# Opening of a convolution-attention hybrid: where its 0/1 blocks, first constants, weight products and shift rows are handled

## The chip, the cores and the metric

One core of a Trainium2 chip. The metric is the device time of one execution in microseconds. TensorE does matrix products into PSUM, ScalarE activations and copies, VectorE elementwise work and reductions, GpSimd (POOL) fills and casts, SyncE (SP) issues DMAs; ScalarE can issue DMAs too. Each engine runs its own instructions in order and waits for others at semaphores.

## The reference

The input is `x`, 4 images of 64 channels by 1,024 positions. Layer 0 is per image, over the 1,024 positions as tokens:

```
x_ln = layernorm(x over channels) * ln1_w + ln1_b
q, k, v = x_ln @ qkv_w            # 4 heads of 16
x = x + proj(softmax(q k^T / 4) v) + proj_b
x = x + fc2(gelu(fc1(layernorm(x) * ln2_w + ln2_b)))
```

Layer 1 takes the result `t` as tokens: a second attention of 8 heads of 64 over a sliding window of 32 tokens, `t + (attention @ Wu^T + bu)`, then a batch-normed linear layer with a recurrence over the images' tokens, `y = sigmoid(wx + y V^T)`, added to `t`. In layer 1 the products of weights `Wq^T Wk` and `Wv^T Wu^T` are formed once for each head and used in place of the four matrices.

## The kernel before

**Tiling.** Channels lie on partitions, and an image's 1,024 positions are two halves of 512 columns, one on partitions 0 to 63 and one on 64 to 127. Matmuls have 512 columns. PSUM has eight banks: `T` (three), `O`, `R` (four).

**The attention of layer 0.** Keys and queries are split in three bf16 parts (`qk_part`), and rows of these parts are stacked to 96 rows (`KX`, `QX`), so that one bf16 matmul gives scores near fp32. For each image and half a first pass computes all scores only for their row maxima (`max_piece`: a matmul at L795 into a bank of a ring, a VectorE reduction at L1308), 32 pieces with 8 for each head. `max_end` then negates (`max_neg`), transposes (`max_rows`, L804) and splits the maxima in three parts (`max_parts`); SyncE copies those to three more rows of `QX` (`shift_rows`, L607 to L612, three transfers), where rows of ones in `KX` add them to the scores. Then `scores` (L815), the exponential on ScalarE (L1146) and `values` (L830) run over 16 key blocks (`u`) and 4 heads.

**The opening.** Image 0 has no time for a trip through DRAM, so `relay` (L774) stacks its rows with matmuls against 0/1 blocks `sel`, which ScalarE makes in twelve copies of `eye` (L1216 to L1219). SyncE issues image 0, `first` (all constants that layer 0 opens with, 714 columns), `early`, `rest`, and the other images (L577 to L581). POOL fills `eps`, `sel` with zeros, the value tiles `VT` with zeros and then ones, others, and the rows of ones in `KX` (L646 to L659); ScalarE waits for the fifth of these that is counted before its table load (L1212). The norm is `ln_mean` (L721), `ln_square` (L1104), `ln_var` (L727, L1109, L1111), `ln_scale` (L1270). Filler matmuls (`keep_clock`, L696) stand before waits of TensorE: seven at the very start, five before the first `ln_var`, eight before the first projection. The projection (L741) is evicted by ScalarE at L1122. Images 1 to 3 have their rows split by POOL and stacked through DRAM (`relayout`, L583).

**Products.** `products` forms two folded bias columns, the products of `Wq`, `Wk` into `R` (`abd`), those of `Wv`, `Wu` into `O` (`gbd`), and a third folded column; ScalarE copies them out.

**The order.** One list, `timeline`, names all steps, and each engine runs those that it has. `order_of_stages` writes it: the opening by hand (L219 to L223), with the relay of the next head after piece 3 of each head and `products` at that place of the last; then the 284 steps of `attend_stages` of four images, among which tables of places put the maxima of the next half (`MAX_AT`), all steps of layer 0's rest and layer 1 (`LAYER_AT`, in quarters of a step), and the end (`END_AT`, `UNIFY_AT`). A plan of the PSUM ring (`plan_ring`) follows from the list.

## Time and profile before

| | us |
|---|---|
| median of 3 runs | 460.96 |
| lowest, highest | 454.33, 461.22 |
| the profiled execution | 458.44 |
| its span | 456.5 |
| TensorE busy | 413.2 |
| VectorE busy | 296.7 |
| ScalarE busy | 296.3 |
| POOL busy | 42.3 |

The span runs from the first to the last instruction of one profiled execution; 1.9 us of its time lie around it. Timelines and windows count from the span's start. A row of a timeline merges equal neighbours (`x7`), and the bracket at its end is the idle time of that engine before it and what ended it. An fp32 matmul is recorded as two instructions.

### The profile page before, as it was taken

The numbers are of one execution on the slowest core, as the hardware profiler recorded it, in microseconds if no ns is written. First come the engines' busy times: TensorE is split into PE (matmuls) and PEld (weight loads), VectorE is DVE, ScalarE is ACT, GpSimd is POOL, SyncE is SP. The second block draws the span as 40 slices with busy tenths as digits, with TensorE's granted clock in tenths as the row PEclk, the third lists the DMA queues.
The fourth block names the chain that finished last, engine by engine and source line by source line (L and its number), as shares of the span: only waits on it lengthen the run. The fifth ranks groups of instructions, "written<-read, shape, count | busy, mean of one in ns | idle before, by whom it ended". The sixth has DMA issues, their size and how long they took to land.

```text
span 456.5 us, 7908 instructions
## 1 busy us (share of the span) xinstructions
PE 413.2 (91%) x3210; PEld 156.6 (34%) x3210; DVE 296.7 (65%) x541; ACT 296.3 (65%) x512; POOL 42.3 (9%) x57
## 2 busy tenths in 40 slices
PE   6787999999999999999999999899999988897893
PEld 2335232322322433232224433232134322453492
DVE  1696795989998746579885556997042644625424
ACT  3442577758788477587876675779977756264551
POOL 9300110003003000012031000000300000100000
PEclk9997699999999999999999999999999999799997
DMA  7300065001810000005500000000000000000003
GB/s 294 99 1 1 3 130 79 12 2 23 183 16 1 14 1 1 1 13 128 81 3 13 1 1 3 12 2 1 1 3 1 0 1 0 3 1 2 1 1 93
DMA packets 7158, 14.02 MB, mean 31 GB/s; under 512 B 1872, under 2 KB 4176, under 8 KB 6992
## 3 DMA queue, kind: packets, MB, share of 16 engines
q1 hardware_dynamic: 7120, 13.50, 12.7%
q8 instruction: 26, 0.43, 0.4%
q14 instruction: 12, 0.10, 0.1%
HBM read 9.20 MB, written 3.41 MB: 28 GB/s over the span
## 4 chain that ended last, share of the span: by engine, by line
PE 63%; ACT 15%; DVE 13%; issue 3%; DMA 3%; POOL 2%; SPq 1%; DVEq 0%; ACTq 0%; POOLq 0%
PE O L830 10%; PE T L815 5%; DVE part_max L1308 5%; PE T L795 5%; ACT z L1169 4%; PE R L815 3%; PE R L727 3%; PE R L999 3%; PE R L886 3%; PE R L795 3%; PE R L960 3%; PE R L721 2%; PE R L987 2%; DMA KX<-qk_scratch 2%; PE R L974 2%
## 5 line engine op out<-in xcount | busy, mean ns | idle before, releaser
L1308 DVE TENSOR_REDUCE part_max<-T 128x1 f32<-128x512 f32 x164 | 105.7, 683 | 23.4 <-PE T L795 23.1
L1146 ACT ACTIVATE probs<-T 128x512 f32<-128x512 f32 x146 | 81.3, 601 | 23.4 <-PE T L815 23.1
L1146 ACT ACTIVATE probs<-R 128x512 f32<-128x512 f32 x110 | 62.2, 599 | 19.2 <-PE R L815 18.9
L830 PE MATMUL O<-probs,VT 128*32 128x512 f32 x512 | 67.6, 603 | 0.3 <-ACT probs L1146 0.2
L1308 DVE TENSOR_REDUCE part_max<-R 128x1 f32<-128x512 f32 x92 | 60.7, 683 | 10.0 <-PE R L795 9.5
L795 PE MATMUL T<-KX,QX 96*128 96x512 bf16 x164 | 57.0, 393 | 4.6 <-DVE part_max L1308 3.0
L815 PE MATMUL T<-QX,KX 99*128 99x512 bf16 x146 | 49.6, 384 | 1.8 <-DVE part_max L1308 1.3
L815 PE MATMUL R<-QX,KX 99*128 99x512 bf16 x110 | 38.1, 382 | 0.6 <-DVE qk_rest L1285 0.4
L672 POOL CAST zs<-z 128x512 bf16<-128x512 f32 x28 | 17.2, 614 | 200.6 <-ACT z L1169 200.6
L795 PE MATMUL R<-KX,QX 96*128 96x512 bf16 x92 | 32.7, 387 | 1.8 <-DMA KX<-qk_scratch 0.9
L1177 ACT ACTIVATE p<-R 128x1024 f32<-128x1024 f32 x14 | 14.3, 1024 | 26.7 <-PE R L960 26.7
L795 PEld LDWEIGHTS T<-KX,QX 96*128 96x128 bf16 x164 | 15.0, 99 | 47.8 <-DVE part_max L1308 18.6
L1169 ACT ACTIVATE z<-R 64x512 f32<-64x512 f32 (+1 forms) x44 | 26.2, 596 | 5.6 <-PE R L886 4.6
L815 PEld LDWEIGHTS T<-QX,KX 99*128 99x128 bf16 x146 | 12.6, 97 | 38.1 <-ACT probs L1146 12.5
L1430 DVE TENSOR_TENSOR zs<-R,rden 128x512 f32<-128x512 f32 x24 | 15.4, 685 | 13.4 <-PE R L987 13.4
L1104 ACT ACTIVATE ln_q<-R 128x512 f32<-128x512 f32 (+1 forms) x14 | 8.2, 589 | 20.6 <-PE R L721 20.6
L886 PE MATMUL R<-xp,abd 64*64 64x512 f32 x128 | 17.2, 613 | 2.4 <-ACT z L1169 2.1
L1184 ACT ACTIVATE rlog<-R 128x1024 f32<-128x1024 f32 x16 | 16.3, 1020 | 4.7 <-PE R L974 4.6
L830 PEld LDWEIGHTS O<-probs,VT 128*32 128x32 f32 x512 | 10.3, 108 | 26.4 <-issue 15.8
L1400 DVE TENSOR_REDUCE neg_m<-R 128x16 f32<-128x576 f32 x16 | 12.1, 758 | 10.5 <-PE R L921 10.5
L815 PEld LDWEIGHTS R<-QX,KX 99*128 99x128 bf16 x110 | 9.7, 97 | 24.5 <-issue 6.4
L727 PE MATMUL R<-ln_q,s_first 128*128 128x512 f32 (+1 forms) x28 | 16.1, 660 | 2.1 <-ACT ln_q L1104 2.1
(241 smaller groups left out, 592.8 us busy)
## 6 DMA issues: line engine op xcount, KB each, us to landing
qk_scratch<-qk_part SPq DMA_DIRECT2D x12, 192.0 KB, 3.0
zs<-early SPq DMA_DIRECT2D x1, 2048.0 KB, 8.4
QX<-qk_scratch SPq DMA_DIRECT2D x6, 256.0 KB, 5.4
KX<-qk_scratch SPq DMA_DIRECT2D x6, 256.0 KB, 5.7
result<-probs SPq DMA_DIRECT2D x2, 512.0 KB, 5.1
s_rest<-rest SPq DMA_DIRECT2D x1, 946.0 KB, 11.1
X<-x SPq DMA_DIRECT2D x2, 384.0 KB, 12.6
QX<-qk_scratch SPq DMA_DIRECT2D x6, 128.0 KB, 5.5
```

The lines of the kernel that those rows point to most:

```text
L672: nc.gpsimd.tensor_copy(*z_cast_of(h)).then_inc(g["z_cast"], 1)
L727: mm(ln_bank(b, which, i, 1), t["mean_c"], ln_bufs(b, which, i)["ln_q"], start=True, stop=True).then_inc(g["ln_var"], 1)
L795: mm(ring["max_piece", b, half, i], QX[b % 2][0:KQ, half, h, nt * P:(nt + 1) * P], KX[b % 2][0:KQ, kh, h, :], start=True, stop=True).then_ ...
L815: mm(ring["scores", b, u, h], KX[b % 2][:, j // QT, h, j % QT * P:(j % QT + 1) * P], QX[b % 2][:, half, h, :], start=True, stop=True).then ...
L830: last = mm(O[h * HP:(h + 1) * HP, :], VT[b % 2][:, j, h, :], probs[:, u % 2, h, :], start=(j == 0), stop=(j == KT - 1))
L886: last = mm(R[half_rows(half ^ odd), (h + odd) % z_banks(b), :], abd[half_rows(half), h + odd, half_rows(half)], xn[half_rows(half), :], s ...
L1146: A(probs[:, u % 2, h, :], ring["scores", b, u, h], ACT.Exp, scale=HD ** -0.5).then_inc(g["exp_done"], 1)
L1169: last = A(dst, ps, ACT.Copy)
L1177: A(p1[:, r % 2, :, :], s1_bank(b, r), ACT.Exp).then_inc(g["p1_exp"], 1)
L1184: A(rlog[:, :, :], den1_bank(b, r), ACT.Ln).then_inc(g["den1_log"], 1)
L1308: nc.vector.tensor_reduce(part_max[:, row, kh:kh + 1], ring["max_piece", b, half, i], AX_X, ALU.max).then_inc(g["max_red"], 1)
L1430: last = TT(cols, pv1_bank(b, r)[odd].rearrange("p (k h q) -> p k h q", k=PPS, h=H1), rden1(b, r)[:, odd, :].rearrange("p (k h q) -> p k h ...
```

## The change

- The twelve copies that make the 0/1 blocks go from ScalarE's start to behind its last activation of the first norm (`rows_of_parts`).
- `first` is cut in two: `first` (`mean_c`, `center`, vectors; 266 columns), issued by ScalarE, and `second` (`eye`, `wq`, `wk`, `wv`; 448 columns), issued by SyncE at the old place. TensorE waits for `second` before the bias matmuls.
- ScalarE's table load waits for one POOL fill instead of five. The two zero fills of `VT` go; POOL's counts fall by two.
- Two filler matmuls instead of five stand before the first `ln_var`.
- `products` is two steps. The first (two folds, `abd`) stands after the fourth piece of the last head instead of the third, the second (`gbd`, last fold) after the eighth.
- The shift rows of a half go in one transfer instead of three.
- The four tables of places have new values (the first of each is shown).

```diff
-FIRST = {"mean_c": P, "center": P, "vectors": len(VECTORS), "eye": C, "wq": P, "wk": P, "wv": P}
+FIRST = {"mean_c": P, "center": P, "vectors": len(VECTORS)}
+SECOND = {"eye": C, "wq": P, "wk": P, "wv": P}
...
 MAX_AT = (
     (
-        0, 0, 0, 0, 1, 1, 1, 6, 6, 7, 8, 8, 10, 10, 11, 12, 13, 15, 15, 15, 15, 16, 21, 21, 21, 21, 21, 22, 24, 29, 34),
+        0, 0, 1, 1, 2, 3, 4, 4, 6, 7, 7, 7, 7, 10, 10, 13, 13, 15, 16, 18, 18, 18, 18, 18, 18, 18, 18, 25, 29, 29, 33),
...
 LAYER_AT = (
-    0, 0, 0, 2, 5, 5, 15, 320, 320, 320, 322, 332, 335, 339, 344, 344, 346, 359, 383, 396, 405, 406, 411, 413,
+    0, 0, 0, 3, 9, 9, 17, 320, 320, 320, 323, 324, 333, 341, 344, 344, 346, 357, 373, 397, 408, 408, 413, 415,
...
-        out += [*pieces[:RELAY_AT], ("relay", 0, h + 1) if h + 1 < H0 else ("products",), *pieces[RELAY_AT:]]
+        out += [*pieces[:RELAY_AT], *([("relay", 0, h + 1), *pieces[RELAY_AT:]] if h + 1 < H0 else [pieces[RELAY_AT], ("products", 0), *pieces[RELAY_AT + 1:], ("products", 1)])]
...
             load_x(0, 1, "x0_in")
-            sp.dma_start(pack["first"][:], a["first"]).then_inc(g["first_in"], 16)
+            sp.dma_start(pack["second"][:], a["second"]).then_inc(g["second_in"], 16)
             sp.dma_start(pack["early"], a["early"]).then_inc(g["early_in"], 16)
...
-                for p in range(PARTS):
-                    sp.dma_start(QX[b % 2][KQ + p:KQ + p + 1, half, :, :].rearrange("o h (t n) -> o (h t) n", n=P),
-                                 mx_part[p * ROWS:(p + 1) * ROWS, :]).then_inc(g["shift_in"], 16)
+                sp.dma_start(QX[b % 2][KQ:KQ + PARTS, half, :, :].rearrange("p h (t n) -> p (h t) n", n=P),
+                             mx_part[:, :]).then_inc(g["shift_in"], 16)
...
             for i in range(2):
-                nc.gpsimd.memset(VT[i][:], 0.0).then_inc(g["pool_fills"], 1)
-            pool.wait_ge(g["pool_fills"], 3)
-            for i in range(2):
                 nc.gpsimd.memset(VT[i][:, :, :, HD:HP], 1.0).then_inc(g["pool_fills"], 1)
...
                 if which == 1 and b < 1:
-                    keep_clock(5)
+                    keep_clock(2)
...
                 if b < 1:
                     keep_clock(8)
+                    pe.wait_ge(g["second_in"], 16)
...
+            def rows_of_parts():
+                act.wait_ge(g["sel_zero"], 1)
+                act.wait_ge(g["second_in"], 16)
+                for q in range(2):
+                    for i, r in enumerate(PART_OF_ROW[q]):
+                        last = A(sel[:, q, r, i, :], t["eye"], ACT.Copy)
+                last.then_inc(g["sel_done"], 1)
...
                 A(buf["ln_r"], buf["ln_l"], ACT.Exp, scale=-0.5).then_inc(g["ln_rstd"], 1)
+                if (b, which) == (0, 1):
+                    rows_of_parts()
...
-            act.wait_ge(g["pool_fills"], 5)
+
+            act.dma_start(pack["first"][:], a["first"]).then_inc(g["first_in"], 16)
+            act.wait_ge(g["pool_fills"], 1)
             nc.scalar.preload_act_table_set("natural_log_exp_and_others")
-            act.wait_ge(g["sel_zero"], 1)
-            act.wait_ge(g["first_in"], 16)
-            for q in range(2):
-                for i, r in enumerate(PART_OF_ROW[q]):
-                    last = A(sel[:, q, r, i, :], t["eye"], ACT.Copy)
-            last.then_inc(g["sel_done"], 1)
```

## Rows read from the trace of the kernel before

**Rows 1.** The page: TensorE's busy tenths in 40 slices, then its granted clock.

```profile
PE   6787999999999999999999999899999988897893
...
PEclk9997699999999999999999999999999999799997
```

**Rows 2.** Window 80 to 380 us: busy (instructions) of PE, PEld, DVE, ACT, POOL; clock.

```profile
80.00:380.00 300.00, 286.58 (x2216) 93.97 (x2213) 208.85 (x369) 221.28 (x357) 21.66 (x32) 1.00 0.10 20
```

**Rows 3.** Chain of waits, opening: start, length, what.

```profile
6.93 1.86 ACT z L1218 x12
...
22.37 12.06 DVE part_max L1308 x20
```

**Rows 4.** Timeline of TensorE, 0 to 11 us: start, length, instruction, idle before.

```profile
1.99 3.01 PE L700 MATMUL T<-abd 128*128 128x512 bf16 x7 [1.99 <-DVE abd L1452]
5.95 1.10 PE L721 MATMUL R<-X,s_first 128*128 128x512 f32 x2 [0.95 <-DMA s_first<-first]
6.89 1.24 PE L700 MATMUL T<-abd 128*128 128x512 bf16 x5
9.33 1.13 PE L727 MATMUL R<-ln_q,s_first 128*128 128x512 f32 x2 [1.20 <-ACT ln_q L1104]
```

**Rows 5.** Timeline of ScalarE, 0 to 16 us.

```profile
5.64 1.28 ACT L1213 ACT_TABLE_LOAD   x1 [5.64 <-POOL VT L652]
...
8.70 0.57 ACT L1104 ACTIVATE ln_q<-R 128x512 f32<-128x512 f32 x1
...
13.97 1.27 ACT L1122 ACTIVATE qk_part<-R,qk_bias 128x512 bf16<-128x512 f32 x2 [2.13 <-PE R L741]
```

**Rows 6.** Timeline of POOL: the first fill that is counted.

```profile
0.74 0.10 POOL L646 MEMSET eps<- 128x1 f32 x1 [0.29 <-POOLq L1605]
```

**Rows 7.** DMA issues: KB each, median us from issue to landing.

```profile
s_first<-first SPq DMA_DIRECT2D x1, 357.0 KB, 3.8
X<-x SPq DMA_DIRECT2D x2, 128.0 KB, 2.7
```

**Rows 8.** Timeline of TensorE, 34 to 50 us.

```profile
34.71 0.34 PE L1017 MATMUL R<-s_first 128*128 128x1 f32 x2
...
36.94 1.93 PE L1027 MATMUL O<-zs 128*64 128x64 f32 x32
...
43.01 0.66 PE L804 MATMUL T<-s_rest,neg_max 128*48 128x128 f32 x2 [2.40 <-DVE neg_max L1313]
...
45.28 1.92 PE L721 MATMUL R<-X,s_first 128*128 128x512 f32 x2
47.88 2.07 PE L727 MATMUL R<-ln_q,s_first 128*128 128x512 f32 x2 [0.69 <-ACT ln_q L1104]
```

**Rows 9.** Timeline of VectorE, 34 to 41 us.

```profile
34.94 1.88 DVE L1308 TENSOR_REDUCE part_max<-T 128x1 f32<-128x512 f32 x3
39.47 0.69 DVE L1308 TENSOR_REDUCE part_max<-R 128x1 f32<-128x512 f32 x1 [2.65 <-PE R L795]
```

**Rows 10.** Windows of 2 us, columns as in rows 2.

```profile
34.00:36.00 2.00, 1.79 (x22) 1.41 (x23) 2.00 (x4) 0.32 (x2) 0.00 (x0) 0.86 0.00 0
...
38.00:40.00 2.00, 2.00 (x23) 1.22 (x20) 0.53 (x1) 1.48 (x3) 0.00 (x0) 0.79 0.00 0
...
42.00:44.00 2.00, 0.99 (x3) 0.37 (x4) 1.20 (x5) 0.00 (x0) 0.00 (x0) 0.57 0.00 0
```

**Rows 11.** Shift: issue, waiting matmul, queue from 44 to 50 us, landing; TensorE's waits.

```profile
100.85 1.79 SPq L611 DMA_DIRECT2D QX<-mx_part  x3
...
103.84 0.61 PE L815 MATMUL R<-QX,KX 99*128 99x512 bf16 x2 [0.20 <-DMA QX<-mx_part]
...
q1 hardware_dynamic: 96, 0.01, 1.2%
...
QX<-mx_part SPq DMA_DIRECT2D x3, 4.0 KB, 1.8
...
PE R L795 <- DMA KX<-qk_scratch: 0.9, 1, 0.9
```

## The prediction and its working

> **What bounds the kernel.** I read the page's slices first. From the fifth to the thirty-sixth TensorE is busy 8 or 9 tenths of each; the first four and the last four are looser, and the granted clock is down in slices four and five (34 to 57 us) and near the end [rows 1]. A window puts a number on the middle: between 80 and 380 us TensorE stands idle 300 - 286.6 = 13.4 us, with VectorE busy 209 of 300 [rows 2]. So the middle is a full TensorE queue, which passes on whatever happens ahead of it: what the opening gains, the end gains. The change works on the opening (0 to 53 us), and there the chain of waits says what sets the time: ScalarE's twelve copies are on it, then the first norm, and from 22.4 to 34.4 us VectorE's row maxima, back to back [rows 3]. The timelines fill in the rest, with what each engine waited for.
>
> **Start of the first norm.** TensorE's seven filler matmuls end at 5.00 us; it then waits 0.95 us for the first constants, and centres the image at 5.95 us [rows 4]. ScalarE can't use that at once: it waits for POOL's fifth counted fill until 5.64, loads its table for 1.28, makes the twelve 0/1 blocks (1.86 us) and squares at 8.70 us [rows 3, 5]. TensorE stands 1.20 us before the variance matmul at 9.33 [rows 4]. The change does three things here.
> First, the copies go behind the norm's second activation. Second, the table load waits for one POOL fill, done at 0.84 us, not for five [rows 6]. Third, `mean_c`, `center` and the vectors (266 of 714 columns, 136 KB of 357 KB) leave on ScalarE's own queue while SyncE issues the image. Today they are issued third, at 5.84 - 3.8 = 2.04 us; the two 128 KB image halves, of the same size and issued before that, land 2.7 us after issue, so by 4.7 us [rows 4, 7]. ScalarE has nothing else to do, so it issues near 0.8 us, as POOL's first fill starts; I expect the 136 KB near 0.8 + 2.7 = 3.5 us and bound it by 0.8 + 3.8 = 4.6. All are inside the fillers, so the centring starts at 5.00. It takes 1.10 us; the square takes 0.57 and TensorE starts 0.06 us behind it (9.33 - 9.27), with as much ahead of it. The variance matmul starts at 5.00 + 1.10 + 0.04 + 0.57 + 0.05 = 6.76 against 9.33: **2.57 us**. Five fillers take 1.24 us [rows 4], so two take 0.5 and end inside the 0.66 us in between: the smaller number costs nothing.
> The copies now lie between the norm's last activation and the first projection eviction at 13.97, an idle of 2.13 us in which VectorE scales and TensorE projects [rows 5]. They take 1.86: 0.27 us of slack, and beyond it only the excess would cost. Their reader, the relay, stands behind that eviction and two VectorE steps. `wq`, `wk`, `wv`, `eye` (229 KB) hold SyncE's old third place and land by 5.8 us as the bigger transfer does now; their first reader, the bias matmuls, stands behind eight fillers after 6.76 + 1.1 us. SyncE issues as many as before. The two full fills of `VT` go; POOL sets nothing in the opening but the table load. Bounds of this part: 0.95 us less if the constants are as late as now; 0.8 us less if TensorE's matmuls are still slow at 5.0 us (the seven fillers take 0.43 us each, the next five 0.25 [rows 4]).
>
> **Products of weights.** They now stand after three pieces of the last head's maxima. From 34.71 us on folds and `abd` take 2.23 us, then `gbd` 1.93, then the last fold about 0.3 [rows 8]. VectorE, back to back so far, runs out at 36.82 and waits 2.65 us [rows 9]. After the change a fourth piece goes ahead, into the bank that VectorE leaves at about 35.0, then folds and `abd` until 37.5, and the next piece is there at 37.9. VectorE has four pieces, until 36.82 + 0.6 = 37.4: it waits 0.5 us, not 2.65. That is **2.1 us** (2.65 if `abd` runs at full clock). The `gbd` part follows the eighth piece. TensorE now stands 2.40 us behind that piece, for VectorE's maxima and `neg_max` [rows 8]; after the change VectorE has four pieces until 37.9 + 2.4 = 40.3 and the negation until 40.7, and TensorE works until 40.3 to 40.5, so nothing is added. At half clock pieces and `gbd` end near 41.5, 0.8 us too late: then the term is 1.3. ScalarE's copies of `gbd`, which the second norm waits for through the last fold, end about 1.5 us after TensorE's part, at 41.9, and that norm would start near 42.2; behind them ScalarE has only that norm.
>
> **The clock.** Behind the 2.40 us of idle the granted clock falls: 0.57 in the window from 42 to 44 us [rows 10], and slice five (to 57 us) shows 6 tenths [rows 1]. Transposing and four pieces take 45.28 - 43.01 = 2.27 us here, the centring 1.92 and the variance 2.07 [rows 8], where the first norm has 1.10 and 1.13 at full clock [rows 4]. At twice the clock the first would be up to 1.1 shorter; I take 0.8, since the ring's fourth bank is held by the transposed maxima until VectorE has read it. Sum: 0.8 + 0.82 + 0.94 = **2.6 us**. With the gap filled by `gbd`, I take the clock to stay up: it rose within 38 to 40 us, right after products and folds alone [rows 10], and was at full from slice one to three with pieces and relay. Against it: it fell within 34 to 36 us, where TensorE was busy 1.79 of 2 us [rows 10].
>
> **Shift transfer.** SyncE issues three today, over 1.79 us, and the last lands 103.84 - 100.85 = 2.99 us after the first issue. TensorE is idle for it there for 0.20 us [rows 11]; I saw no other place in the waits. One transfer has the same 48 pieces of 256 bytes; it lands 1.8 us after issue plus what its spread costs. The four denominator transfers queued behind it on SyncE go 1.2 us sooner. At most **0.2 us**, and not below -1.
> The spread: three issues moved 96 packets in 1.2% of 16 engines' 6.0 us [rows 11], or 1.15 us, 24 ns for each that carries data. If one transfer ran on three engines, 16 would stand in a row: 0.4 us, landing at 2.2 us, still 0.8 sooner. The Trainium skill, DMA: Bandwidth & Descriptors, section "Why a DMA increments its semaphore by 16 and not by 1", speaks against the edit: the engines used are the largest number that divides the slowest dimension of both sides, by which this one has 3 of 16 (3 and 48), and each of today's three has 16. With the row's price the sum by that rule keeps its 0.2; no run here shows it yet.
>
> **Orders.** The tables of places move most maxima and layer steps of the middle by a few places. Counts are the same. There are 13.4 us of idle to win from or add to; I take 0 and bounds of 3 either way. The wait of 0.9 us for the keys of image 1 [rows 11] stays, since both its sides move together; the projection is placed one score later, 0.2 to 0.4 us.
>
> **Sum.** The profiled execution took 458.44 us, 456.5 of it span, 0.5% under the median of 460.96; one of three runs was at 454.33. 458.44 - 2.57 - 2.1 - 0.2 - 2.6 = 451.0 us.
>
> **Rivals.**
> - The clock falls all the same. For it: it fell once in a busy stretch. Then 458.44 - 2.57 - 1.3 - 0.2 = 454.4 us.
> - The gain is taken back in the middle: TensorE is early at some transfer or VectorE (209 of 300 us busy, but near its limit wherever maxima stand close) has no room. The wait for the keys of image 1 would grow, or the orders lose 3 us: 455 to 460, say 457.
> - Orders that also win: 3 us more, 448. For it, the 13.4 us; against it, that is 4% of 300 and split over many waits.
> - The other side, slower than before: the new order misplaces maxima so that TensorE stands before VectorE's banks between 80 and 380 us. Idle there would have to go from 13.4 to above 21 us to use up the 7.5 gained, and to 33 us for 2% slower. A wait there is a VectorE reduction's length, 0.6 us (12.06 for 20 [rows 3]), so it takes 13 of them to lose the gain; at 18 the time is 462 us.
> - The one transfer is served by three engines, and a packet in a row costs far more than 24 ns: at 0.13 us each (an assumed price) it lands at 1.8 + 16 x 0.13 = 3.9 us, 0.9 later than today, and TensorE waits that at the one place: 451.0 + 0.2 + 0.9 = 452.1 us. The page of the Trainium skill just named would bring it about.
>
> **Chances.** My sum 0.48; clock falls 0.22; taken back 0.12; orders win 0.10; slower 0.05; three engines dear 0.03. The likeliest one's own range is 448.5 to 453.5. For 8 in 10, I go from 447.5 (the winning orders, nearly whole) to 457.5 (half of what is taken back). A change of 2%, about what a measurement of this kernel can tell from none, is 9.2 us: below 451.7. A bit over half of the sum's case (0.28), the winning orders (0.10) and a little of the three-engine one (0.01) lie there: 0.39. Slower by over 2% (470.2) keeps 0.03, the rest 0.58.
>
> **What would show it.** Centring at 5.0 and variance matmul at 6.8 us; ScalarE's twelve copies before an eviction at 11.4; VectorE's gap in the last head at most 0.6 us; `neg_max` near 38.1; no granted clock of 0.50 from 40 to 50 us, and a second norm whose matmuls take 1.1 each; the variance matmul of the second norm near 41.6, not 47.9. Wrong would be: constants landing after 5.0, idle in 80 to 380 us far from 13.4, or the shift waited for by more than 1 us.

## The result, and the profile after

The changed kernel takes 451.25 us (median of 4 runs, 450.95 to 452.19). The kernel before, run beside it on the same chip, took 461.09 us (four runs, 454.33 to 462.95). The ratio is 0.9894 with an interval of [0.9848, 0.994]: 1.1% faster, and the same within 2%. A ratio leaves out executions more than 1.5% above a kernel's fastest, here two of before's four (461.22 and 462.95), so that one of the two left is its shortest, 454.33; the medians of all four differ by 9.84 us, 2.1%.

The time itself came out as predicted (451.0), the change of it did not: -2.2% was forecast against the median of three, -1.1% measured. A second comparison, below (six runs beside eleven of before), gave 0.9847 [0.9801, 0.9894]. Beside the experiments before ran 83 times (453.05 to 462.84, median 458.3), and the changed kernel ran 10 times in all (448.99 to 453.89, median 451.3): 7.0 us, or 1.5%, less. Whether one reads 1.1, 1.5 or 2.1% depends on which runs of before one meets, and that is the subject of what follows.

The page of the changed kernel, TensorE's busy tenths and granted clock in 40 slices. Slices four and five are up against [rows 1]; the fall near the end is still there.

```profile
PE   7789999999999999999999999899999888897893
...
PEclk9998999999999999999999999999999999699997
```

TensorE of the changed kernel in the opening, answering to [rows 4]: start, length, instruction, idle before. Then ScalarE, answering to [rows 5].

```profile
1.99 3.17 PE L697 MATMUL T<-abd 128*128 128x512 bf16 x7 [1.99 <-DVE abd L1462]
4.95 1.91 PE L718 MATMUL R<-X,s_first 128*128 128x512 f32 x2
...
7.55 1.13 PE L724 MATMUL R<-ln_q,s_first 128*128 128x512 f32 x2
```

```profile
0.74 0.38 ACTq L1227 DMA_DIRECT2D s_first<-first  x1
1.15 1.28 ACT L1229 ACT_TABLE_LOAD   x1 [1.15 <-POOL eps L646]
...
9.97 1.85 ACT L1108 ACTIVATE z<-s_second 128x64 bf16<-128x64 f32 x12
12.19 1.27 ACT L1133 ACTIVATE qk_part<-R,qk_bias 128x512 bf16<-128x512 f32 x2 [0.37 <-PE R L739]
```

The centring starts behind the fillers without a wait, at 4.95, and the variance matmul at 7.55, where it was at 9.33. The centring took 1.91 us, not 1.10, as a matmul of its size does at half clock. (The granted clock of the windows says 1.00 in these first microseconds all the same, in every profile here, so the mean granted clock used below doesn't count a slow start.) The twelve copies run at 9.97, and the eviction behind them still waits 0.37 us for TensorE, so they cost nothing.

TensorE and VectorE of the changed kernel at the last head and the second norm, answering to [rows 8] and [rows 9].

```profile
34.10 1.73 PE L1022 MATMUL R<-zs 128*64 128x64 f32 x32
...
37.58 1.26 PE L1028 MATMUL O<-zs 128*64 128x64 f32 x32
...
39.35 0.42 PE L802 MATMUL T<-s_rest,neg_max 128*48 128x128 f32 x2 [0.20 <-DVE neg_max L1323]
...
40.75 1.08 PE L718 MATMUL R<-X,s_first 128*128 128x512 f32 x2
42.51 1.13 PE L724 MATMUL R<-ln_q,s_first 128*128 128x512 f32 x2 [0.69 <-ACT ln_q L1113]
```

```profile
34.95 0.68 DVE L1318 TENSOR_REDUCE part_max<-R 128x1 f32<-128x512 f32 x1
36.41 1.89 DVE L1318 TENSOR_REDUCE part_max<-T 128x1 f32<-128x512 f32 x3 [0.77 <-PE T L793]
...
38.92 0.37 DVE L1323 TENSOR_REDUCE neg_max<-part_max 128x16 f32<-128x32 f32 x3
```

VectorE waits 0.77 us where it waited 2.65, TensorE 0.20 where it waited 2.40, and the second norm's matmuls take 1.1 us each where they took 1.92 and 2.07. Its variance matmul stands at 42.51, before at 47.88.

Windows of the changed kernel, columns as in [rows 2]. The clock still falls at `abd`, as it did before (0.61 from 34 to 36 us; 0.86 and then 0.50 in before); from 42 to 44 us it is full, where before had 0.57. The middle has 15.8 us of idle against 13.4.

```profile
34.00:36.00 2.00, 2.00 (x35) 1.75 (x35) 1.63 (x3) 0.46 (x3) 0.00 (x0) 0.61 0.00 0
...
42.00:44.00 2.00, 1.49 (x5) 0.68 (x6) 1.60 (x4) 0.78 (x2) 0.00 (x0) 1.00 0.03 6
...
80.00:380.00 300.00, 284.20 (x2200) 93.86 (x2200) 204.81 (x364) 220.60 (x354) 22.45 (x33) 1.00 0.09 19
```

The shift transfer, answering to [rows 11]: its issue on SyncE, the weight load that waits for it, and the hardware queue from 40 to 46 us, in which one shift is sent.

```profile
93.12 0.78 SPq L611 DMA_DIRECT2D QX<-mx_part  x1
```

```profile
95.41 0.23 PEld L813 LDWEIGHTS R<-QX,KX 99*128 99x128 bf16 x2 [0.54 <-DMA QX<-mx_part]
```

```profile
q1 hardware_dynamic: 51, 0.01, 0.9%
```

It lands by 95.41, 2.29 us after its issue (before 2.99); the forecast for three engines was 2.2.

### The profile page after: what moved, and what is told of

The parts are those of the page before. It is cut to its first block, busy times and chain, and to the rows that moved or that the text cites. A ratio compares the mean times of both kernels' runs of the same rounds, so it can differ in the third digit from the quotient of the medians.

```text
span 449.2 us, 7886 instructions
## 1 busy us (share of the span) xinstructions
PE 410.0 (91%) x3207; PEld 155.4 (35%) x3207; DVE 296.0 (66%) x541; ACT 296.4 (66%) x512; POOL 40.7 (9%) x55
## 4 chain that ended last, share of the span: by engine, by line
PE 66%; ACT 18%; DVE 12%; issue 3%; DVEq 0%; ACTq 0%
PE O L828 11%; PE T L813 6%; DVE part_max L1318 5%; ACT z L1182 5%; PE T L793 5%; PE R L813 4%; ACT probs L1159 4%; PE R L793 4%; PE R L997 3%; PE R L958 3%; PE R L718 3%; PE R L724 3%; PE R L884 2%; PE R L985 2%; PE R L972 2%
## 5 line engine op out<-in xcount | busy, mean ns | idle before, releaser
L1318 DVE TENSOR_REDUCE part_max<-T 128x1 f32<-128x512 f32 x160 | 103.1, 681 | 16.7 <-PE T L793 16.3
L1159 ACT ACTIVATE probs<-T 128x512 f32<-128x512 f32 x151 | 84.4, 599 | 20.7 <-PE T L813 20.2
L1159 ACT ACTIVATE probs<-R 128x512 f32<-128x512 f32 x105 | 59.5, 601 | 20.1 <-PE R L813 19.5
L1318 DVE TENSOR_REDUCE part_max<-R 128x1 f32<-128x512 f32 x96 | 62.8, 681 | 4.6 <-PE R L793 4.4
L793 PE MATMUL T<-KX,QX 96*128 96x512 bf16 x160 | 55.0, 387 | 4.4 <-DVE part_max L1318 2.1
L813 PE MATMUL T<-QX,KX 99*128 99x512 bf16 x151 | 51.8, 383 | 2.3 <-DVE part_max L1318 2.3
L813 PE MATMUL R<-QX,KX 99*128 99x512 bf16 x105 | 36.2, 382 | 0.0
L813 PEld LDWEIGHTS T<-QX,KX 99*128 99x128 bf16 x151 | 13.4, 97 | 41.3 <-DVE part_max L1318 16.5
L972 PE MATMUL R<-p,s_rest 64*64 64x512 f32 x128 | 17.0, 599 | 0.8 <-ACT rlog L1197 0.4
```

Of the source, the lines that this page charges most:

```text
L793: mm(ring["max_piece", b, half, i], QX[b % 2][0:KQ, half, h, nt * P:(nt + 1) * P], KX[b % 2][0:KQ, kh, h, :], start=True, stop=True).then_ ...
L813: mm(ring["scores", b, u, h], KX[b % 2][:, j // QT, h, j % QT * P:(j % QT + 1) * P], QX[b % 2][:, half, h, :], start=True, stop=True).then ...
L972: last = mm(den1_bank(b, r)[half_rows(half), odd, :], t["block_ones"][half_rows(odd), :], p1[half_rows(odd), r % 2, half, :], start=True, ...
L1159: A(probs[:, u % 2, h, :], ring["scores", b, u, h], ACT.Exp, scale=HD ** -0.5).then_inc(g["exp_done"], 1)
L1318: nc.vector.tensor_reduce(part_max[:, row, kh:kh + 1], ring["max_piece", b, half, i], AX_X, ALU.max).then_inc(g["max_red"], 1)
```

## The experiments

All times are in us. "At equal clock" is explained under the second group. The short names in bold are used afterwards.

### Each part alone

**Start alone**: before, with the two transfers, the copies behind the norm, one fill awaited, POOL's two zero fills gone, and two fillers.

```diff
-FIRST = {"mean_c": P, "center": P, "vectors": len(VECTORS), "eye": C, "wq": P, "wk": P, "wv": P}
+FIRST = {"mean_c": P, "center": P, "vectors": len(VECTORS)}
+SECOND = {"eye": C, "wq": P, "wk": P, "wv": P}
...
-                    keep_clock(5)
+                    keep_clock(2)
...
+                if (b, which) == (0, 1):
+                    rows_of_parts()
...
+            act.dma_start(pack["first"][:], a["first"]).then_inc(g["first_in"], 16)
+            act.wait_ge(g["pool_fills"], 1)
```

> The kernel before with the first part alone: constants in two transfers, copies behind the norm's second activation, table load after one fill, two fillers; products, shift and places as before. By my sum the variance matmul of the first norm starts 1.8 to 2.6 us sooner and the whole kernel ends that much sooner: 456 us against a profiled 458.4. The clock's fall behind the idle stretch at 40 us stays. The rival (the part is given back in the middle) says no change.

454.85 (452.29 to 459.82, 10 runs), ratio 0.9946 [0.9898, 0.9994]. In its profile the centring takes 1.30, the variance matmul starts at 6.94 (2.39 earlier), and nothing else changes: the gaps of 2.65 and 2.40 us are there, and the clock falls behind them as before. TensorE, and the window from 42 to 44 us:

```profile
40.61 0.66 PE L803 MATMUL T<-s_rest,neg_max 128*48 128x128 f32 x2 [2.40 <-DVE neg_max L1324]
...
42.89 1.91 PE L719 MATMUL R<-X,s_first 128*128 128x512 f32 x2
```

```profile
42.00:44.00 2.00, 2.00 (x5) 0.82 (x3) 1.96 (x5) 0.00 (x0) 0.00 (x0) 0.50 0.01 2
```

**Products alone**: before, with the products in two parts.

```diff
-        out += [*pieces[:RELAY_AT], ... else ("products",), *pieces[RELAY_AT:]]
+        out += [*pieces[:RELAY_AT], ... else [pieces[RELAY_AT], ("products", 0), *pieces[RELAY_AT + 1:], ("products", 1)]]
```

> The kernel before with the products in two parts and nothing else. By my sum VectorE's gap in the last head falls from 2.65 to at most 0.8 us and TensorE's idle before the transposed maxima from 2.40 to under 0.5 us; the clock then stays up in the second norm, whose centring takes 1.1 instead of 1.9 us: 2.1 + 2.6 = 4.7 us less than the profiled before, near 453.7. The rival (the clock falls all the same) says 2.1 or less, 456 to 457, with 0.50 in the windows of 42 to 50 us.

452.82 (451.25 to 454.73, 4 runs), ratio 0.9891 [0.9783, 0.9998]. Run again:

> The kernel before with the products in two parts, once more. By the traces of the run with the gap filled, VectorE's gap at full clock is 1.14 us, not 2.65; so the split is worth 0.5 to 0.9 us against runs of before at the same clock, and the rest of its gain is that its clock stays up more often: mean clock above 0.98 in most runs, median 453 to 454.5. My recorded terms (2.1 at equal clock) say 2 us under before's runs of the same clock.

454.01 (451.09 to 457.58, 12 runs), ratio 0.9914 [0.9879, 0.9949]. VectorE, then TensorE, of the first of the two:

```profile
40.87 1.29 DVE L1313 TENSOR_REDUCE part_max<-T 128x1 f32<-128x512 f32 x2 [1.15 <-PE T L795]
```

```profile
38.32 1.98 PE L1024 MATMUL R<-zs 128*64 128x64 f32 x32
...
43.82 0.42 PE L804 MATMUL T<-s_rest,neg_max 128*48 128x128 f32 x2 [0.59 <-DVE neg_max L1318]
...
45.22 1.07 PE L721 MATMUL R<-X,s_first 128*128 128x512 f32 x2
```

TensorE waits 0.59 us, not 2.40, and the second norm runs at full clock. VectorE's gap was to be at most 0.8 us and is 1.15, with the first part of the products at half clock (1.98); in the second of the two profiles, at full clock, it has none. TensorE and the second norm do what was expected, start or no start.

**New opening, old places** (the changed kernel with the four tables of before), and **old opening, new places** (the reverse):

```diff
-MAX_AT, LAYER_AT, END_AT, UNIFY_AT as in the changed kernel
+MAX_AT, LAYER_AT, END_AT, UNIFY_AT as in the kernel before
```

> The changed kernel with the four tables of places of the kernel before. My sum puts nothing on the tables: 451 to 452 us, as the changed kernel. If the tables carry part of the gain, it is slower than the changed kernel by that part; the wait for the keys of image 1 near 70 us, gone in the changed kernel, would be back with 0.9 us.

453.14 (450.24 to 455.58, 4 runs), ratio 0.9885 [0.9779, 0.9992]. Its profiled execution is its longest, 455.58, with a mean clock of 0.973. TensorE never waits ahead of the transposing there, and yet it is at half clock from the products to the second norm's centring:

```profile
40.15 0.66 PE L802 MATMUL T<-s_rest,neg_max 128*48 128x128 f32 x2
...
42.42 1.59 PE L718 MATMUL R<-X,s_first 128*128 128x512 f32 x2
```

```profile
38.00:40.00 2.00, 2.00 (x34) 1.88 (x32) 1.41 (x5) 0.25 (x1) 0.00 (x0) 0.50 0.01 4
```

> The kernel before with the new tables of places alone. My sum: no change (within 1 us of before). If the tables alone gain, up to 1 to 2 us less than before.

457.57 (455.94 to 461.26, 10 runs), ratio 1.0011 [0.9967, 1.0056]. The profiled execution of this one matters later: its opening is before's, instruction for instruction up to the last head, with a mean clock of 0.979. TensorE, VectorE, and a window:

```profile
35.29 1.15 PE L1022 MATMUL R<-zs 128*64 128x64 f32 x32
36.27 1.10 PE L1027 MATMUL O<-zs 128*64 128x64 f32 x32
...
41.51 0.42 PE L804 MATMUL T<-s_rest,neg_max 128*48 128x128 f32 x2 [2.40 <-DVE neg_max L1313]
```

```profile
37.96 0.69 DVE L1308 TENSOR_REDUCE part_max<-R 128x1 f32<-128x512 f32 x1 [1.14 <-PE R L795]
```

```profile
42.00:44.00 2.00, 2.00 (x6) 0.67 (x4) 1.90 (x6) 0.00 (x0) 0.00 (x0) 0.73 0.00 0
```

TensorE was at full clock at the products here, undivided as they are. They take 1.15 and 1.10 us, not the 1.88 and 1.93 of before's profile [rows 8], and VectorE waits 1.14 us for them, not the 2.65 of [rows 9]. The clock falls only later, behind the 2.40 us of idle.

Then the first of the two again:

> The changed kernel with the tables of places of before, once more with more rounds (4 runs gave 450.2 to 455.6). My sum: within 0.5 us of the changed kernel in the median. The rival (the new places carry part of the gain) says 1 us or more slower, as the wait for the keys of image 1 comes back.

451.51 (448.73 to 455.79, 6 runs), ratio 0.9824 [0.9771, 0.9877]. So the new tables gain nothing: alone they change nothing in the ratio, and the new opening is at least as good without them, though TensorE then does stand for the keys of image 1 (TensorE of the first run with the old places; no matmul of the changed kernel has such a wait):

```profile
72.33 0.60 PE L793 MATMUL R<-KX,QX 96*128 96x512 bf16 x2 [1.43 <-DMA KX<-qk_scratch]
```

### Filling TensorE's gap without moving anything

The runs of each kernel of the first group spread by 3 to 8 us, and so the spread was larger than the effects. It isn't the chip: before ran beside the others on five of them, with medians from 457.9 to 458.5 and 5.8 us or more from lowest to highest on each. Sorted by the mean granted clock that each run shows, before's 83 runs fall almost on a line (some of the clocks):

| mean granted clock | runs of before | median us |
|---|---|---|
| 0.987 | 4 | 453.2 |
| 0.983 | 5 | 455.1 |
| 0.980 | 4 | 455.7 |
| 0.975 | 12 | 456.9 |
| 0.972 | 9 | 458.1 |
| 0.968 | 13 | 459.6 |
| 0.965 | 3 | 460.8 |
| 0.964 | 7 | 461.1 |
| 0.961 | 1 | 462.8 |

The line through all 83 has a slope of -0.34 us for each 0.001 of clock, with 0.47 us of scatter around it. A kernel's distance to this line, at its own clock, is what it gains "at equal clock"; the rest of its gain is a higher clock. The two add up to the whole by the way they are defined, and the line credits a higher clock wherever it is gained, also where it buys no time. Only 10 of the 83 runs have 0.983 or more; the profiled one has 0.972, the median. If the gap ahead of the second norm makes the difference, ten fillers in it should bring the long runs down and leave the shortest alone.

**Gap filled**: before, with ten dependency-free matmuls on data of the kernel ahead of the wait for `neg_max`.

```diff
             def max_rows(b, half):
 
+                if b == 0 and half == 0:
+                    pe.wait_ge(g["abd_done"], 4)
+                    keep_clock(10, pack["rest"][:, 0:256].bitcast(BF16), O[:, :])
                 pe.wait_ge(g["negmax"], 2 * b + half + 1)
```

> The kernel before with ten filler matmuls into bank O while TensorE waits for the negated maxima of the first half (2.40 us of idle at 40.6 us); nothing else changed. If the idle stretch is what lets the clock fall there, the clock stays at full from 40 to 53 us, the second norm's centring takes 1.1 instead of 1.9 us, and the kernel is 2 to 2.6 us shorter than before though no work moved. If the clock's fall has another cause, the windows still show 0.50 and the time is that of before or up to 0.5 us more.

454.86 (453.36 to 456.53, 8 runs), ratio 0.9938 [0.9899, 0.9977]; before had 458.21 beside it (25 runs, 453.19 to 461.61). The median is 3.3 lower, the fastest run is not; at equal clock it is 0.4 worse, though in the profile the fillers delay nothing (the transposing starts at 41.49, with the gap left idle at 41.51). The spread is down from 8.4 in 25 runs to 3.2 in 8. Its TensorE:

```profile
38.98 2.33 PE L700 MATMUL O<-s_rest 128*128 128x512 bf16 x10
...
42.89 1.08 PE L721 MATMUL R<-X,s_first 128*128 128x512 f32 x2
```

**Start filled** and **both filled**: 9 and 10 fillers around the first norm where before has 7 and 5; and both together.

```diff
-            keep_clock(7)
+            keep_clock(9)
...
-                    keep_clock(5)
+                    keep_clock(10)
```

> The kernel before with nine fillers instead of seven at the start and ten instead of five before the first variance matmul, so that TensorE never waits long in the first 9 us. The runs of before lie between 454 and 463 us, those of the changed kernel within 1.3 us. Theory: before's spread comes from where the clock rises in an opening with two idle stretches; then this kernel's highest run comes down by some us and its median is below that of before by 1 to 3 us. Rival: the spread comes from the later fall of the clock or from transfers; then the spread stays 5 us and more.

458.83 (453.24 to 461.44, 12 runs), ratio 0.9984 [0.9949, 1.002].

> Both sets of fillers. If the clock alone makes the spread, this one has runs within 1.5 us of one another and a median near the lowest run of before, 454 us. If not, the spread stays.

455.13 (453.52 to 459.34, 12 runs), ratio 0.9948 [0.9916, 0.9981]. Filling around the first norm brings nothing; filling the gap ahead of the second brings 3 us on the median. The runs with both filled were to lie within 1.5 us of one another and span 5.8, so that gap is a large source of the spread and not the only one. The profiles show two more. With the start filled, with both filled and in the first run of products alone the clock goes to half between 20 and 21 us, for 3 to 4 us, while TensorE relays the second head. In five profiles (start alone, gap filled, products alone again, three shifts, and one of the last group) it is at half for 3 to 4 us between 288 and 296. Neither is in the profiles of before or of the changed kernel. Both filled, then gap filled:

```profile
22.00:24.00 2.00, 2.00 (x9) 0.53 (x6) 0.43 (x2) 1.20 (x3) 0.00 (x0) 0.50 0.00 0
```

```profile
292.00:294.00 2.00, 2.00 (x12) 0.52 (x12) 1.93 (x4) 1.23 (x4) 0.00 (x0) 0.50 0.00 0
```

The profiles put the stretches side by side. The first goes from the first norm's variance matmul to the transposing of `neg_max`, the second from there to the second norm's variance matmul; the last column is from the same transposing to the projection of image 1.

| profile | products | clock at products | first stretch | second stretch | to projection |
|---|---|---|---|---|---|
| before | undivided | half (1.88, 1.93) | 33.68 | 4.87 | 9.44 |
| start alone | undivided | half (1.98, 1.80) | 33.67 | 4.88 | 9.42 |
| start filled (half clock at the relay) | undivided | half (1.78, 1.93) | 35.29 | 4.87 | 9.43 |
| old opening, new places | undivided | full (1.15, 1.10) | 32.18 | 4.08 | 8.69 |
| gap filled | undivided | full (1.15, 1.10) | 32.16 | 3.17 | 6.55 |
| both filled (half clock at the relay) | undivided | full (1.15, 1.10) | 33.29 | 3.17 | 6.55 |
| changed | divided | half, then nearly full (1.73, 1.26) | 31.80 | 3.16 | 6.55 |
| three shifts | divided | half (1.98, 1.97) | 32.94 | 3.23 | 6.62 |
| new opening, old places | divided | half (1.98, 1.98) | 32.96 | 4.54 | 7.93 |
| products alone (half clock at the relay) | divided | half, then full (1.98, 1.15) | 34.11 | 3.16 | 6.54 |
| products alone, again | divided | full (1.15, 1.15) | 31.01 | 3.16 | 6.55 |
| tail filled (below) | divided | full (1.15, 1.15) | 31.00 | 3.17 | 6.55 |

Dividing saves 33.68 - 32.94 = 0.7 us with both at half clock and 32.17 - 31.01 = 1.2 with both at full; the clock at the products saves 1.5 by itself undivided and 1.9 divided. Half clock at the relay costs 1.6 (start filled against before) or 1.1 (both filled against gap filled). In all four profiles that keep the gap the clock falls behind it; with the gap filled, by fillers or by `gbd`, the way to the projection is 2.1 to 2.9 us shorter in every profile but one. That one is the new opening with old places: its clock was down at the products and came up only at 43 us.

### The shift transfer

**Three shifts**: the changed kernel with before's three transfers.

```diff
-                sp.dma_start(QX[b % 2][KQ:KQ + PARTS, half, :, :].rearrange("p h (t n) -> p (h t) n", n=P),
-                             mx_part[:, :]).then_inc(g["shift_in"], 16)
+                for p in range(PARTS):
+                    sp.dma_start(QX[b % 2][KQ + p:KQ + p + 1, half, :, :]..., mx_part[p * ROWS:(p + 1) * ROWS, :])
```

> The changed kernel with three shift transfers a half, as before. My sum gives the single transfer 0.2 us: this one is 0 to 0.3 us slower than the changed kernel. The rule that a transfer of 3 rows is served by three engines says the single one lands with 16 packets in a row; the trace of the changed kernel against this one shows whose last packet comes sooner after the first issue (three: 2.99 us).

451.95 (450.94 to 454.58, 6 runs), ratio 0.9849 [0.9812, 0.9886]. The changed kernel again, later:

> The changed kernel itself, next to the kernels beside it. Theory (a run's time is set by where its clock is down): its runs lie 4 us under runs of before that have the same mean granted clock (0.983: 455 for before, 451 for this), and its fastest runs show a clock of 0.98 and more. The ratio to before lies between 0.984 and 0.990. If the clock did not matter, runs of equal clock would differ as widely as all do.

451.98 (448.99 to 453.89, 6 runs), ratio 0.9847 [0.9801, 0.9894]. The waits for this transfer differ as expected (the page's waits: total, times, longest; three transfers first, then one), and no difference in time is to be seen. (Before has such waits of its weight loads too, 1.4 and 0.9 us; the prediction counted the matmul's 0.20 alone.)

```profile
PEld R L814 <- DMA QX<-mx_part: 1.8, 2, 1.2
...
PEld T L814 <- DMA QX<-mx_part: 1.0, 2, 0.8
```

```profile
PEld T L813 <- DMA QX<-mx_part: 0.8, 1, 0.8
...
PEld R L813 <- DMA QX<-mx_part: 0.5, 1, 0.5
```

### Towards a better kernel

**Tail filled**: the changed kernel, with fillers ahead of and between the window products of the last image, where the clock falls in every kernel above. **Early and tail**: that, with TensorE starting 0.8 us sooner and a filler behind each of three pieces of the last head.

```diff
                 for k in range(2):
+                    if b == B - 1:
+                        keep_clock(1, ones16)
                     bank = win_bank(b, r)[:, k, :]
...
                 if r == 0:
+                    if b == B - 1:
+                        keep_clock(6, ones16)
                     pe.wait_ge(g["xbd_cast"], b + 1)
```

> The changed kernel with six filler matmuls before and one within each of the eight window groups of the last image, where every run so far shows 7 to 10 us of half clock. If the idle and the small matmuls there let the clock fall, it stays up longer and the kernel is 1 to 2.5 us shorter than the changed one; if not, the fillers cost up to 1 us.

452.17 (451.79 to 455.81, 6 runs), ratio 0.9875 [0.9831, 0.9919].

> The same with two more edits in the opening: the fill that the first fillers read is cut, so that TensorE starts at about 1.3 instead of 2.0 us and centres the first image near 4.5 instead of 5.0; and one filler behind each of three pieces of the last head. Theory: 0.5 to 1 us less than the kernel with the tail filled alone. Rival: the image lands too late for that, no difference.

452.11 (450.85 to 453.10, 6 runs), ratio 0.9844 [0.9806, 0.9882]. TensorE of the changed kernel, whose clock falls at 386 us, and then of the tail filled:

```profile
384.54 0.28 PE L915 MATMUL R<-win_mask 4*128 4x288 bf16 x1 [1.44 <-DVE zs L1393]
...
387.66 0.43 PE L919 MATMUL R<-xbd,zs 128*32 128x72 bf16 x16
...
390.70 1.17 PE L930 MATMUL R<-s_rest,neg_m 128*96 128x128 f32 x4
```

```profile
383.30 0.32 PE L923 MATMUL R<-xbd,zs 128*32 128x72 bf16 x16
383.55 0.39 PE L697 MATMUL T<-unit_sel 112*128 112x512 bf16 x1
...
390.34 0.68 PE L934 MATMUL R<-s_rest,neg_m 128*96 128x128 f32 x4 [0.44 <-DVE neg_m L1420]
```

The fillers hold the clock, and the products take 0.32 us instead of 0.43, but from the first mask to `neg_m` it is 390.34 - 383.08 = 7.3 us with them and 390.70 - 384.54 = 6.2 without, at half clock. A filler of 0.2 to 0.4 us per group of 0.3 costs more than the clock gives. This kernel also shows what "at equal clock" leaves out: its mean clock is up to a median of 0.989, its time isn't down, and by the line it would stand 3 us behind the changed kernel.

**Last head filled**: only the three fillers in the last head, in the changed kernel; then the same with the **old places**; then with the **early start and six** fillers ahead of the last windows.

```diff
                    start=True, stop=True).then_inc(g["max_mm"], 1)
+                if hn == 0 and 25 <= i <= 27:
+                    pe.wait_ge(g["lay_in"], LAID)
+                    keep_clock(1, zeros16, O[:, :])
```

> The changed kernel with one filler matmul behind each of the second, third and fourth piece of the last head, where TensorE stands between VectorE's reductions; no fillers in the tail. Theory: the clock's fall at 35 us (the products at half clock) goes away; the median comes down by 0.5 to 1 us against the changed kernel (452.0), and high runs become rarer. Rival: no difference, since the fall depends on more than these gaps.

451.00 (448.71 to 452.29, 6 runs), ratio 0.9833 [0.9791, 0.9874].

> The same with the tables of places of the kernel before. If the places carry nothing at equal clock, it equals the one with the new places within 0.5 us, and its runs at a mean clock of 0.990 are near 448.8, as those of the changed kernel with old places.

449.75 (449.16 to 452.93, 6 runs), ratio 0.982 [0.9777, 0.9862].

> The changed kernel with the earlier start (fill of abd cut), the three fillers of the last head, and six fillers before the window groups of the last image but none within them. In the run with fillers within the groups, the windows took 7.3 us instead of 6.2 though at full clock. Theory: without those eight the windows end sooner and the early start is worth 0.5 us: 449 to 450 us. Rival: the fillers before the groups hold the windows up too, and nothing is won against the changed kernel.

449.92 (448.74 to 453.93, 6 runs), ratio 0.981 [0.9771, 0.9849]. TensorE and VectorE of the second, in which `abd` runs at full clock and VectorE has hardly a gap (34.85 + 0.68 to 35.67):

```profile
34.16 1.15 PE L1025 MATMUL R<-zs 128*64 128x64 f32 x32
```

```profile
34.85 0.68 DVE L1321 TENSOR_REDUCE part_max<-R 128x1 f32<-128x512 f32 x1
35.67 1.89 DVE L1321 TENSOR_REDUCE part_max<-T 128x1 f32<-128x512 f32 x3
```

**Early start added to it**: `abd`'s fill in two parts, so that TensorE's fillers start at 1.19 us instead of 1.99.

```diff
-nc.vector.memset(abd[:], 0.0).then_inc(g["fills"], 1)
+nc.vector.memset(abd[:, 0:2, :], 0.0).then_inc(g["fills"], 1)
+nc.vector.memset(abd[:, 2:, :], 0.0).then_inc(g["fills"], 1)
```

> The changed kernel with the earlier start (fill of abd cut in two), the three fillers of the last head and the places of before. Each was measured in another mix: old places 0.5 us less at equal clock, fillers of the last head 0.5 to 1 us, the early start unknown alone. Theory: 449.0 to 449.5 us in the median, with most runs at a mean clock of 0.987. Rival: the early start brings nothing (the image is there, but TensorE's slow first matmuls only start slower), 449.8 as without it.

450.35 (448.83 to 454.41, 6 runs), ratio 0.9836 [0.9788, 0.9885]. It centres at 4.28 and has its variance matmul at 6.16, 1.39 us ahead of the changed kernel's, and no gain is to be told from the kernel without it. The early start isn't sure either: in the profile of early start and six, TensorE waits 0.50 us for the image and has its variance matmul at 7.63. The best of these kernels (449.75) is 1.5 us under the changed one's 451.3, with an interval that overlaps its own.

## Why the prediction was right in its time and wrong in its change

Of profile against profile the sum held: -2.57 - 2.1 - 0.2 - 2.6 = -7.47 was worked out, and the profiled executions are 458.44 and 450.95, -7.49. Of it 52.45 - 45.90 = 6.55 us are there when the projection of image 1 starts (before's and the changed kernel's rows below); the last 0.9 come behind it, and no run says from what. By its steps:

- **Start, 2.57.** Constants in time: the 133 KB are issued at 0.74 and take 2.3 us, so they land at 3.0 (I had 3.5). Copies hidden, two fillers inside the square's time: right. The term was 1.78 in the profile, since the centring was at half clock, the bound of 0.8 that the prediction named; 2.39 in the start-alone profile; 2.2 at equal clock over its 10 runs. Somewhat too large. The centring behind the same seven fillers took 1.17, 1.30, 1.55 and 1.91 us in four profiles (three shifts; start alone; new opening, old places; changed), so this term too is one of an execution.
- **Products, 2.1.** `neg_max` was forecast at 38.1 and starts at 38.92, all of which is the late start. From the first variance matmul to `neg_max`, before has 42.58 - 9.33 = 33.25 us and the changed kernel 38.92 - 7.55 = 31.37: 1.9 less. As a comparison of two executions it was right. As a price of the part it was mis-sized: 0.7 to 1.2 in the table above, and 0.8 at equal clock over 16 runs (0.4 in four, 0.9 in twelve).

VectorE of before, the negation that this term and the next start from:

```profile
42.58 0.37 DVE L1313 TENSOR_REDUCE neg_max<-part_max 128x16 f32<-128x32 f32 x3
```

- **Clock, 2.6.** From `neg_max` to the projection of image 1 it is 52.45 - 42.58 = 9.87 against 45.90 - 38.92 = 6.98: 2.9. The clock did stay up there, with `gbd` in the gap. The rival in which it falls all the same isn't out for all executions: in one of six profiles with this opening and no fillers in the last head (new opening, old places) it was at 0.50 from 36 to 42 us, with TensorE busy throughout.

TensorE, the projection's first matmuls, before and after:

```profile
52.45 1.09 PE L741 MATMUL R<-x_ln,s_first 64*64 64x512 f32 x8
```

```profile
45.90 1.09 PE L739 MATMUL R<-x_ln,s_second 64*64 64x512 f32 x8
```

- **Shift, 0.2.** Three engines serve it, as the packets count: 51 are its 48 pieces and one more for each of three, where [rows 11] had 96 for three transfers, 48 and 16 for each. By the Trainium skill, DMA: Bandwidth & Descriptors, section "Why a DMA increments its semaphore by 16 and not by 1", that is what 3 and 48 leave; the trace agrees with 51. The rival built on it priced a packet at 0.13 us and had it land after 3.9; the trace has 2.29 us, and the 24 ns of [rows 11] gave 2.2. That rival is out. In the time it is worth nothing that can be measured (451.95 and 451.98).
- **Orders, 0.** Within its bounds of 3, but the new places lose a little wherever the two sets were compared at equal clock: 0.9 us with the old opening, 0.5 with the new one (10 runs against 10), 0.8 with the last head filled. The profiles agree in sign: the idle of TensorE from 80 to 380 us is 15.8 in the changed kernel and 15.3 in the same with old places, 14.8 with the old opening and new places and 13.4 in before. So the 15.8 come in part from the tables and in part from the opening. "Orders win" is out, and of "taken back in the middle" this is a small piece. The wait for the keys, which was to stay, is gone and was worth nothing.

**The step that failed** is the one that says how the profiled execution stands to the runs, and with it the two terms that depend on it. I priced products (2.1) and clock (2.6) on an execution with a clock of 0.972, in which TensorE was slow at the products and behind the gap, noted that one of three runs was at 454.33, and took the difference for noise. It is the same thing that the change removes. The old opening has executions in which the clock is up at the products (old opening, new places; gap filled; both filled), and there the gap that the division closes is 1.14 us and not 2.65. That in before's fastest ones (0.983 and more) it doesn't fall behind the idle either was not seen in a trace; it is read from the table of clocks and from the gap filled, which reaches the same time and clock as they do. Against these the change has little to win: 3.1 us at equal clock, 0.7%. (The start's 2.2 and the products' 0.8 make 3.0, but the tables take 0.5 to 0.9 off again; the parts are known to some 0.3 each, and what fills the rest is not shown.) Against its typical ones it wins the clock too: a median of 0.9825 for 0.972 is 10.5 x 0.34 = 3.6 us. The two make 6.7 of the 7.0 measured, as they must by their definition; the independent check is the gap filled, which without any work moved takes 3.3 us off the median, with its clock up from 0.972 to 0.983. So products alone are worth 458.3 - 454.0 = 4.3 us on the median over their 16 runs, close to the 4.7 that my two terms make; but by the line that is 0.8 of order and 3.5 of clock.

The forecast of -2.2% then came from setting 451.0 against 460.96, a median of three that is 2.6 us above before's own over 83 runs; my own sum against the profiled execution was -1.6%, and 1.5% is what the medians of all runs show. The first ratio's -1.1% in turn leans on before's run at 454.33. That 451.0 met the time within 0.3 us is in part luck: its first three terms put 7.3 us ahead of the projection, the profiles show 6.55 there, and the changed kernel's own runs go from 449.0 to 453.9. Before's 83 runs show it as a mixture from 453 to 463 us: 451.0 is 0.5% under the shortest of them and 2.6% under the longest, so "within 2%" deserved far more than 0.58.

**What stays open.** Why the clock is up at the products in some executions and down in others of the same opening: the work ahead of them is the same. The same goes for the relay behind 20 us and for the place near 290. The Trainium skill, TensorE: Matmul & The Clock Gate, Part 1, says that the same kernel shows different numbers of slow matmuls at its start from run to run; the four lengths of the centring above agree. That is about a kernel's start; for the later places no run here shows what picks the execution. The products' worth at equal clock lies between 0.4 and 0.9. No profile of before itself is at hand with a mean clock other than 0.972. How a lower one can come about is seen in start alone (0.968: products, gap, and near 290) and in start filled (0.964: relay, products, gap). And the fall of the clock near 386 us, in every profile of a kernel without fillers there, wasn't bought off at a profit; real work moved into those 1.44 us of idle wasn't tried.

## What to carry to other kernels

Read the mean granted clock of every run of the kernel before, not of the profiled execution alone. If the time follows it, the kernel is a mixture of executions: price a change once at full clock and once at half, and give the two answers their shares. A stretch priced from rows at half clock, and a term for the clock behind it, are both gains that the executions with the clock up don't have to give. The gap of 2.40 us in an otherwise full TensorE queue was worth filling even with dummy matmuls (3.3 us off the median); real work moved into it did the same, and its median is 0.9 us lower still (454.0 for 454.9). Dummy matmuls between small groups at the end were not.

## What the hardware showed that I had not expected

- The time of before runs on a line with its mean granted clock: 9.8 us from shortest to longest for 0.987 down to 0.961. Ten dummy matmuls in one idle stretch of 2.4 us take 3.3 us off its median.
- The clock falls in some executions and not in others of the same work, also while TensorE is busy: 0.50 from 22 to 24 us (both filled) and from 38 to 40 (new opening, old places), with TensorE busy 2.00 of 2 us in each.
- 32 fp32 matmuls of 64 columns take 1.10 to 1.15 us at full clock and 1.8 to 2.0 at half, so they show the clock well.
- One transfer of 48 pieces of 256 bytes on three engines is issued in 0.78 us and lands after 2.29; three transfers on 16 engines each take 1.79 to issue and land after 2.99.
